# A four-layer graph network: node scaling moved to ScalarE, a softmax with one exchange, empty gather columns left out

## The reference

```python
x = layernorm(x + L0(x))   # gate * segment_sum(h_src - h_dst), gathered again, segment_sum, relu(@W.T + b)
x = layernorm(x + L1(x))   # attention, 1 head, logits with moments (mean, square, cube) of z_src and z_dst over all edges
x = layernorm(x + L2(x))   # attention, 4 heads, self loops, + bias
x = layernorm(x + L3(x))   # relu([x_i, x_j - x_i] @ W1 + b1) @ W2 + b2, segment_max over dst
# attention:
m = segment_max(att, dst); expv = exp(att - m[dst]); denom = segment_sum(expv, dst)
w = expv / denom[dst];     out = segment_sum(w[:, None] * message, dst)
```

```python
mk = mean((z_e - mu) ** k, axis=0); mk = sign(mk) * abs(mk) ** (1 / k)
```

## Time and profile before

| | |
|---|---|
| median of 3 runs | 2642.76 us (2642.62 to 2645.9) |
| profiled execution, time | 2645.48 us |
| its span | 2643.7 us |
| mean granted TensorE clock | 0.748 |
| busy: PE, DVE, ACT, POOL | 53%, 71%, 30%, 55% of the span |
| gathers and scatters | 1200 (600 of them with look_i in layers 0 to 2) |
| HBM traffic | 176 MB, 67 GB/s |

### The profile page before, as it was taken

One profiled execution on the slowest core, in us unless ns is written; L12 is line 12 of the kernel. 1 busy time (PEld: TensorE's weight loads), 2 busy tenths in 40 slices (PEclk: granted clock), 3 DMA queues, 4 the chain that ended last, 5 costly groups with the idle time before them and its releaser, 6 DMA issues. The chain is left out here.

```text
span 2643.7 us, 25893 instructions
## 1 busy us (share of the span) xinstructions
PE 1391.6 (53%) x5742; PEld 830.5 (31%) x5742; DVE 1886.1 (71%) x3916; ACT 792.9 (30%) x1636; POOL 1466.0 (55%) x1409
## 2 busy tenths in 40 slices
PE   1433433334666588886566577633888543333331
PEld 1332333332333344443233454411333222121110
DVE  4877777775777589997688699966888666464542
ACT  0322222222555355654111355521222110010100
POOL 7777777745777576661000577720000277777776
PEclk9655556566877799998688799965889666566666
DMA  4433333331111233332011244420000110101010
GB/s 162 124 107 106 108 107 107 107 84 35 48 48 48 58 101 110 107 106 58 20 38 38 82 130 127 128 63 11 30 26 30 27 22 24 24 23 24 22 22 12
DMA packets 118512, 175.58 MB, mean 66 GB/s; under 512 B 36928, under 2 KB 43182, under 8 KB 118324
## 3 DMA queue, kind: packets, MB, share of 16 engines
q1 hardware_dynamic: 72052, 129.98, 14.7%
q0 software_dynamic: 44800, 44.60, 9.0%
q10 hardware_dynamic: 1600, 0.33, 0.1%
HBM read 89.27 MB, written 86.87 MB: 67 GB/s over the span
## 5 line engine op out<-in xcount | busy, mean ns | idle before, releaser
L447 POOL DMA_INDIRECT GA<-table,look_i x600 | 620.2, 1034 | 509.6 <-PEq L1440 230.1
L1596 POOL DMA_INDIRECT GA<-table,look_i x200 | 205.1, 1025 | 414.3 <-PEq L1670 353.6
L453 PE MATMUL P<-ident,GA 128*128 128x128 f32 x500 | 104.3, 345 | 451.5 <-DMA GB<-in_x,dst_i 213.7
L477 PE MATMUL P<-center,work 128*128 128x128 f32 x800 | 154.1, 355 | 210.7 <-DVE work L1662 175.0
L253 POOL DMA_INDIRECT GA<-in_x,src_i x200 | 217.5, 1087 | 80.4 <-issue 72.2
L1604 POOL DMA_INDIRECT out_x<-work,seg_i x200 | 210.0, 1050 | 61.0 <-issue 60.6
L253 POOL DMA_INDIRECT GB<-in_x,dst_i x200 | 200.8, 1004 | 61.0 <-issue 61.0
L453 PEld LDWEIGHTS P<-ident,GA 128*128 128x128 f32 x500 | 70.4, 174 | 481.8 <-issue 229.7
L495 ACT ACTIVATE work<-P 128x512 f32<-128x512 f32 x100 | 59.8, 598 | 516.4 <-PE P L477 516.3
L477 PEld LDWEIGHTS P<-center,work 128*128 128x128 f32 x800 | 137.5, 259 | 242.3 <-issue 113.7
L596 PE MATMUL P<-center,work 128*128 128x128 f32 x984 | 159.3, 311 | 94.3 <-ACT work L639 68.6
(11 more groups left out here) (320 smaller groups left out, 3454.7 us busy)
## 6 DMA issues: line engine op xcount, KB each, us to landing
table<-work SPq DMA_DIRECT2D x175, 256.0 KB, 2.4
XN<-in_x SPq DMA_DIRECT2D x98, 256.0 KB, 2.7
out_x<-work SPq DMA_DIRECT2D x98, 256.0 KB, 2.1
GA<-table,look_i POOLq DMA_INDIRECT x800
XN<-in_src_pad SPq DMA_DIRECT2D x13, 512.0 KB
cols<-in_dst_pad SPq DMA_DIRECT2D x50, 128.5 KB
table<-XD SPq DMA_DIRECT2D x1, 6400.0 KB
src_wide<-in_src_pad SPq DMA_DIRECT2D x12, 512.0 KB, 5.0
```

The source lines that it names most:

```text
L447: pool.indirect_dma_start(GA[:, par, j * D:(j + 1) * D], None, table_k, bass.IndirectOffsetOnAxis(ap=look[:, s * 8 + j:s * 8 + j + 1], axis=0)
L453: ins = pe.transpose(dst[:, q * 128:(q + 1) * 128], src[:, q * 128:(q + 1) * 128], ident[:, :])
L477: ins = pe.matmul(norm_bank(par, far)[:, q * 128:(q + 1) * 128], W[par][4][:, q * 128:(q + 1) * 128], center[:, :], start=True, stop=True)
L1596: pool.indirect_dma_start(GA[:, par, j * D:(j + 1) * D], None, table[3], bass.IndirectOffsetOnAxis(ap=look_i[:, r * 8 + j:r * 8 + j + 1], ...
```

## The change

It has four parts. Helper names stay; line numbers after it are some 14 to 44 higher.

1. Columns of the last edge tile that hold no edge are neither gathered nor scattered: of its 8 columns 4 are left (0, 2, 4 and 6).
2. In the setup the zeros for the table come from 512 columns, broadcast, instead of from 12800.
3. `softmax_rows` scans upward and downward before the exchange, exchanges both ends at once, and scans again; the result is the maximum of both scans, or their sum less the element. The flags of rows without a break (`whole_runs`) are made once, in the one-head pass. A DMA takes all heads of a part.
4. `biased` is split: the scaling of node tiles is eight Copy activations on ScalarE, one for each row of 64, in node_act2 at yield 3; the bias addition stands in node_dve2 at yield 5. In the first edge stage the scaling stays on VectorE.

```diff
+        def filled(s):
+            return [j for j in range(8) if s * SE + j % 2 * HW + j // 2 * 128 < E]
+        LACK = 16 * (8 - len(filled(NS - 1)))
+        def landed(s, k, passes=1):
+            return k * 128 * passes - (LACK * passes if isinstance(s, int) and s == NS - 1 else 0)
...
-                for j in range(8):
+                for j in filled(s):
...
-                sp.dma_start(table[0][EP:2 * EP, :].rearrange("(p c) f -> p (c f)", p=128), XD[:, :]).then_inc(S("init"), 16)
+                sp.dma_start(table[0][EP:2 * EP, :].rearrange("(s p j) f -> p s (j f)", p=128, j=8),
+                             XN[:, 0:1, :].to_broadcast([128, NS, HW])).then_inc(S("init"), 16)
...
-                pool.memset(XD[:, :], 0.0).then_inc(S("fill"), 1)
+                pool.memset(XN[:, 0, :], 0.0).then_inc(S("fill"), 1)
...
+        def scaled(dve, T, par, k):
+            dve.tensor_tensor(rows(W[par][2]), rows(BN[par][2]), per_row(sm(par, 2)), A.mult).then_inc(T("y0"), 1)
+
         def biased(dve, T, par, k):
             Y = W[par][2]
-            dve.tensor_tensor(rows(Y), rows(BN[par][2]), per_row(sm(par, 2)), A.mult).then_inc(T("y0"), 1)
             dve.wait_ge(T("y0"), k)
...
             double_root(act, T, par, 2, 0, "sd1")
+            yield 3
+            act.wait_ge(T("r1"), k)
+            for j in range(8):
+                part = slice(j * D, (j + 1) * D)
+                ins = act.activation(W[par][2][:, part], BN[par][2][:, part], ACT.Copy, scale=sm(par, 2)[:, j:j + 1])
+            ins.then_inc(T("y0"), 1)
...
             dve.reciprocal(sm(par, 2), sm(par, 2)).then_inc(T("r1"), 1)
-            dve.wait_ge(T("r1"), k)
+            yield 5
             biased(dve, T, par, k)
...
+                def scans(src, up, down, up_mask, down_mask, op0, op1, start, r):
+                    def every(begin_up, begin_down):
+                        for h in range(K):
+                            dve.tensor_tensor_scan(up[:, h, :], up_mask[:, :], src[:, h, :], begin_up(h), op0, op1)
+                        for h in range(K):
+                            ins = dve.tensor_tensor_scan(down[:, h, ::-1], down_mask[:, ::-1], src[:, h, ::-1], begin_down(h), op0, op1)
+                        link(ins)
+                    every(lambda h: start, lambda h: start)
+                    dve.tensor_copy(ends[:, 0:K], up[:, :, RC - 1])
+                    link(dve.tensor_copy(ends[:, HEADS:HEADS + K], down[:, :, 0]))
+                    dve.nop().then_inc(S("ends"), 1)
...
+                    flags = run_rows[0:K, 256 * (r - 1):256 * r]
+                    dve.tensor_tensor_scan(up_in[:, 1:129], flags[:, 0:128], P[0][0:K, 0:128], start, op0, op1)
+                    link(dve.tensor_tensor_scan(down_in[:, 127::-1], flags[:, 255:127:-1], P[0][0:K, 255:127:-1], start, op0, op1))
...
+                    every(lambda h: carry_in[:, h:h + 1], lambda h: carry_in[:, K + h:K + h + 1])
...
-                scan(L, T, row_neg, A.add, A.max, -BIG)
-                spread(T, R)
+                scans(L, T, R, row_neg, row_low, A.add, A.max, -BIG, 1)
+                link(dve.tensor_tensor(R, R, T, A.max))
...
-                scan(X, T, row_same, A.mult, A.add, 0.0)
-                spread(T, R)
+                scans(X, T, R, row_same, row_more, A.mult, A.add, 0.0, 2)
+                link(dve.tensor_tensor(T, T, X, A.subtract))
+                link(dve.tensor_tensor(R, R, T, A.add))
...
+                pool.memset(GA[:, 0, :], 0.0).then_inc(S6("pads"), 1)
+                pool.wait_ge(S6("pads"), 1)
                 gather(0)
```

More of the change, by code:

```diff
@@ L732, in softmax_rows @@
             all_ = lambda m: m[:, :].rearrange("p (o c) -> p o c", o=1).to_broadcast([128, K, RC])
+            by_head = lambda rows_: rows_.rearrange("h (p c) -> p h c", p=128)
+            N_PARTS = 2 + own
             @block.sync
             def _(sp):
[L736 to L739, removed]
+                for t, lo in ((L, 0), (T, K), (LO, 2 * K))[:N_PARTS]:
+                    sp.dma_start(t, by_head(logits[lo:lo + K, :])).then_inc(S("load"), 16)
                 for part in range(PARTS):
[L741 to L746, removed]
+                    sp.wait_ge(S("weights"), part + 1)
+                    sp.dma_start(by_head(weights[part * K:(part + 1) * K, :]),
+                                 half[part].rearrange("p (h c) -> p h c", h=K)).then_inc(S("store"), 16)
+                sp.wait_ge(S("store"), 16 * PARTS)
+            up_in, down_in = carry[0:K, 0:129], carry[0:K, 256:385]
             @block.vector
@@ L755, in link, with whole_runs @@
                     dve.wait_ge(S("dve"), step[0])
[L757 to L767, removed]
+                def whole_runs():
+                    for i, mask in enumerate((row_neg, row_low, row_same, row_more)):
+                        link(dve.tensor_reduce(red[:, i:i + 1], mask[:, :], AX, A.min))
+                        link(dve.tensor_copy(runs[:, i * HEADS:(i + 1) * HEADS], red[:, i:i + 1].to_broadcast([128, HEADS])))
@@ L768, in scan @@
                     dve.nop().then_inc(S("ends"), 1)
+                    dve.memset(up_in[:, 0:1], start)
+                    link(dve.memset(down_in[:, 128:129], start))
                     dve.wait_ge(S("ends_row"), r)
[L770 to L773, removed]
+                    flags = run_rows[0:K, 256 * (r - 1):256 * r]
@@ L780, in spread @@
[L780 to L785, removed]
+                    link(dve.tensor_copy(carry_in[:, 0:2 * K], P[1][:, 0:2 * K]))
+                    every(lambda h: carry_in[:, h:h + 1], lambda h: carry_in[:, K + h:K + h + 1])
+                if not own:
+                    link(dve.tensor_scalar(row_low[:, :], row_more[:, :], -1.0, BIG, A.add, A.mult))
+                    whole_runs()
+                    dve.nop().then_inc(S("runs"), 1)
+                    dve.wait_ge(S("run_rows"), 1)
+                    link(dve.tensor_copy(run_rows, P[2][0:HEADS, :]))
@@ L818, in _ @@
                 if own:
-                    act.activation(XO, LO, ACT.Exp).then_inc(S("exp"), 1)
+                    act.wait_ge(S("own_shifted"), 1)
+                    act.activation(XO, LO, ACT.Exp).then_inc(S("own_exp"), 1)
             @block.tensor
             def _(pe):
-                for r, down in enumerate((False, True, False, True)):
+                if not own:
+                    pe.wait_ge(S("runs"), 1)
+                    for i in range(4):
+                        ins = pe.transpose(P[2][0:HEADS, 128 * i:128 * i + 128], runs[:, HEADS * i:HEADS * (i + 1)], ident[:, :])
+                    ins.then_inc(S("run_rows"), 1)
+                for r in range(2):
                     pe.wait_ge(S("ends"), r + 1)
-                    pe.transpose(P[0][0:K, 0:128], ends[:, 0:K], ident[:, :])
-                    pe.transpose(P[0][0:K, 128:256], ends[:, HEADS:HEADS + K], ident[:, :]).then_inc(S("ends_row"), 1)
+                    for i in range(2):
+                        ins = pe.transpose(P[0][0:K, 128 * i:128 * i + 128], ends[:, HEADS * i:HEADS * i + K], ident[:, :])
+                    ins.then_inc(S("ends_row"), 1)
                     pe.wait_ge(S("carry"), r + 1)
-                    src = carry[0:K, 257:385] if down else carry[0:K, 256:384]
-                    pe.transpose(P[1][:, 0:K], src, ident[0:K, 0:K]).then_inc(S("carry_in"), 1)
+                    pe.transpose(P[1][:, 0:K], up_in[:, 0:128], ident[0:K, 0:K])
+                    pe.transpose(P[1][:, K:2 * K], down_in[:, 1:129], ident[0:K, 0:K]).then_inc(S("carry_in"), 1)
         with nc.Block() as block:
```

39 lines of the change are left out of this document (22 added, 17 removed).

## The result

The changed kernel takes 2744.3 us (median of 4 runs, 2740.3 to 2744.9) against 2644.1 for the kernel before in the same session: a ratio of 1.0375, 95% interval 1.0357 to 1.0393. It is slower by 100 us. The forecast was 2785 in a range of 2735 to 2855. So sign, place and mechanism were right, and the size was taken 41 us too large.

A forecast was written before the change was run, and what follows sets the result against it. POOL was taken to bound the second and third stretches, a ring between DVE and ACT the first. 125 + 56 + 8 - 6 - 5 - 3 - 10 - 16 - 6.7 = +142 gave 2788, on the median 2785 us, range 2735 to 2855.

The forecast's parts named there:

- the ring of ACT and DVE: Both scaled stretches: alternating ACT and DVE waits set the period; 12.52 to 17.7 us in the first (+125), 13.15 second (+56).
- the price of a copy: Start-to-start spacing of ScalarE's 128x64 copies in both scaled stretches: 0.25 us taken, bounds 0.21 and 0.30; eight cost 2.0 us.
- The clock term: Both scaled stretches: a longer period makes PE idler and its clock lower; +0.2 us for each of 46 periods, +8.
- a PEclk under 0.9: Sign that the forecast is wrong: TensorE's granted clock, 1 for 2.4 GHz, falling under 0.9.
- Rival A: Both scaled stretches: the eight copies fall into ACT's idle time, so the kernel is faster, 2563 to 2596 us; chance 0.05.
- rival C: The change does only what its words say, one stage scaled: 2725 us; chance 0.02.
- rival B: Scaled stretches: longer waits drop TensorE to its lower clock (1.2 GHz), much slower, 2815 to 2860 us; chance 0.12.
- The gains: Savings outside the scaled stretches: setup -6, first two gather stages -5 and -3, third stretch -10, softmax -16 and -6.7.
- The setup's term: Setup: without the long memset the gathers start some 7 us earlier (12.4 to about 5); -6, bounds 0 and -10.8.
- The first two gather stages: Stages at 56 to 607 and 615 to 903: empty columns save only what the following wait holds, -5 and -3.
- The two largest terms: ScalarE scaling in the two scaled stretches: +125 in the first, +56 in the second.
- the softmax: Four-head softmax: -16, reduction pair 17.7 to 12.3 us, twelve stores become two; one-head pass: -6.7.

The follow-up runs named there:

- run 1: Changed kernel with the scaling of node tiles back on VectorE in both stretches, bias right behind it: 2584.3 us, 0.979 of the kernel before.
- run 3: Scaling on VectorE in its old place, but the bias addition left at its new place behind the cube: 2621.9 us, 0.9932 of the kernel before.
- run 4: Changed kernel with each of the eight copies issued twice: 2898.1 us; or with one 128x512 copy in place of eight: 2646.0 us.
- run 2: Changed kernel with ScalarE scaling in only one stretch, VectorE in the other: first stretch (S1) only 2700.2 us, second (S4) only 2632.5 us.
- copies-last run: Changed kernel with the eight copies moved behind the square of the side (yield 4.5): 2901.5 us, 1.1001 of the kernel before.
- run 5: Changed kernel with copies moved: behind the side's square, 2901.5 us; or right behind their root, reciprocal ahead of scans, bias ahead of cube, 2782.4 us.
- run 6: Scaling on VectorE, with all eight columns of the last tile gathered and scattered again: 2611.5 us; or with the old memset and clearing DMA: 2592.8 us.

## Why the prediction was right, point by point

- **The mechanism** held: ACT's eight copies lie on the ring of ACT and DVE, and the late bias with them. S1's period 17.09 (17.7 forecast), S4's 12.51 (13.15). Runs 1, 3 and 4 show each term by itself. The reading of the order, that both stretches scale, was right too: run 2 gives 48 us for S4, the part that the few words don't name.
- **The term that was mis-sized is the price of a copy**: 0.25 forecast, 0.196 measured, below what I had called the lower bound (0.21 for 128x8, whose two operations were roots). 16 x 0.054 x 23 = 20 us in each stretch, 40 in all, nearly the whole miss. Beside it the gains came out 7 us larger than forecast, and the other blocks gave 2 us back. The estimate by the Trainium skill, page "ScalarE: Activation LUTs", section "What ACT_TABLE_LOAD costs" (0.24), was 0.04 too high as well. The Trainium skill's section "Rules for kernel authors" on the same page says that plain multiplies belong on VectorE, and this one is cheaper there: 0.69 us against 1.57. But one copy of 128x512 took ScalarE 0.57 us (run 4), so here it is the eight instructions, and not ScalarE's rate, that make it dear.
- **The clock term** of +8 had the right size by luck. With the measured price the two rings come to 16.87 and 12.29 by my sum, and 0.22 us a period, 10 us in all, remains. But ACT waits for PE before L616 once in S1 and twice in S4, and the clock, which did fall (0.96 to 0.79 in S1, 0.95 to 0.88 in S4), has no place on the ring of S1. The ring's steps, each as a mean over the same 16 tiles, show where the 0.22 us lie. In S1 it is the way from the start of the side's square to that of the cube: 2.06 us for the two halves together, where I had 2 x 0.92. 0.09 of it was there before the change, since in every second tile the half with XD takes 1.10 for this and not 0.92, and I had read one tile; why it does, no run shows. Most of the rest is ScalarE's lag behind a series of copies (last section). In S4 it is spread over several steps, the largest 0.08 from the second norm's square to its sums. PE has 0.03 of it: in every third tile the sums L690 start 0.11 us later, behind a square that stands behind the logits, which wait for PE. I had named a PEclk under 0.9 as a sign that the forecast was wrong; that sign was badly chosen. The fallen clock cost next to nothing here, and showed as time where PE was waited for, as in the copies-last run.
- **Rival A** (copies in ACT's idle time) fell with runs 4 and 5, and **rival C** with run 2. Of **rival B** one half came true, the clock fell; but the period went on being ACT's, since with the copies doubled, at 0.81 of the clock in S1, each still cost its own spacing.
- **The gains** were 5.6 + 7.4 + 5.7 + 6.8 + 17.6 + 10.6 = 53.7 us against 46.7. The setup's term held with its reason: the first gather starts at 5.29 us instead of 12.41. The first two gather stages gave 13 instead of 8. I had capped them by the longest wait of each tail, and run 6 shows the columns there to be worth 6.7 and 7.8; what else in those tails moved up was not looked at further. The two largest terms were named in the right order, and the softmax was within 2 us, though two of its steps were wrong: 17.7 us came down to 10.7 and not to 12.3, and the stores became three and not two.

## What to carry to other kernels

An engine's idle time is a place for more work only if it lies at that point of its order. Before moving an operation to a half-idle engine, mark on both engines' timelines which of its operations the other waits for: work put between the awaited input and the awaited output is paid in full, sixteen copies of 0.2 us here as 3.1 us a period, though that engine stood idle over 5 us in the same period.
Moving the work to another point asks for the same reading again, banks included: both re-placements took a resource along (PE's bank, the root before the scans) that cost more than the place saved.
And an edit to a helper touches all stages that call it; the order of the instructions, not the description, says which.

## What the runs showed of the hardware

A series of eight 128x64 ScalarE copies with a column as scale starts one every 0.196 us, though they last from 0.30 us (the first) to 0.35 (the eighth). In the run with sixteen in series the durations grow from 0.29 to 0.42 at constant spacing, and the 128x512 operation behind them lasts 0.71 instead of 0.58:

```profile
1126.35 0.29 ACT L668 ACTIVATE work<-P,small 128x64 f32<-128x64 f32 x1
1126.54 0.30 ACT L669 ACTIVATE work<-P,small 128x64 f32<-128x64 f32 x1
...
1129.30 0.42 ACT L669 ACTIVATE work<-P,small 128x64 f32<-128x64 f32 x1
1129.49 0.71 ACT L616 ACTIVATE work<-P 128x512 f32<-128x512 f32 x1
```

So the starts do not tell when a result is there; it comes later, the longer the series. Who waits for it waits longer too. Behind one copy DVE's cube starts 0.93 us after ACT's square does, behind eight 0.99 (1128.69 to 1129.68 in the rows of the changed kernel above), behind sixteen 1.06. The rows for one and for sixteen:

```profile
1129.37 0.69 ACT L1282 ACTIVATE work<-P,vec 128x512 f32<-128x512 f32 x1
1130.30 0.75 DVE L1212 SCALAR_TENSOR_TENSOR work<-P,vec,work 128x512 f32<-128x512 f32 x1 [1.49 <-ACT work L1282]
...
1130.54 0.82 ACT L1286 ACTIVATE work<-P,vec 128x512 f32<-128x512 f32 x1
1131.60 0.75 DVE L1216 SCALAR_TENSOR_TENSOR work<-P,vec,work 128x512 f32<-128x512 f32 x1 [4.20 <-ACT work L1286]
```

Twice a period that is 0.11 us for the eight copies in means over 16 tiles (2.06 against 1.94), and another 0.14 for the sixteen, which is most of why doubling them cost 3.30 us a period in S1 and not 3.14.
